# Attention on one core: VectorE's share of the softmax summed in quarters, its polynomial in a scratch tensor, row maxima transposed on VectorE and read earlier

## The reference

```
q, k, v = split_heads(xn @ w.T + b, 16 heads of 16)       # q / sqrt(16)
attn    = softmax(q @ k.T) @ v                            # 4096 x 4096 scores per head
out     = x + (attn @ out_w.T + out_b) + fp8_linear(xn)   # both operands rounded to fp8
```

## Time and profile before

| | |
|---|---|
| median of three runs | 1969.61 us |
| the profiled execution's own time | 1972.75 us |
| its span, first to last instruction | 1970.9 us |
| ScalarE busy | 1820.7 us (92%) |
| TensorE busy | 1916.1 us (97%) |
| VectorE busy | 1276.8 us (65%) |
| granted TensorE clock, mean | 0.990 of full speed |

### The profile page before, as it was taken

How to read it: one execution, slowest core, us unless ns; L and a number is a source line. 1 busy time by engine, 2 the same in 40 slices (tenths; PEclk the granted TensorE clock), 3 DMA queues, 4 the chain that set the end, 5 groups by cost and what they waited for, 6 DMA issues and landing times.

```text
span 1970.9 us, 37661 instructions
## 1 busy us (share of the span) xinstructions
PE 1916.1 (97%) x13945; PEld 663.5 (34%) x13945; DVE 1276.8 (65%) x1789; ACT 1820.7 (92%) x2004; POOL 38.1 (2%) x53
## 2 busy tenths in 40 slices
PE   6969999999999999999999999999999999999979
PEld 4623333333333333333333333333333333333327
DVE  6645766656566766657566766667565766666656
ACT  2339999999999999999999999999999999999983
POOL 2000000000000000000000000000000000000000
PEclk9979999999999999999999999999999999999999
DMA  6870121203030121203030121202030121212022
GB/s 197 272 245 8 20 31 25 31 9 47 9 43 13 17 30 25 31 15 41 9 47 9 17 30 25 31 18 38 9 47 9 17 31 25 30 20 36 9 42 86
DMA packets 65622, 83.70 MB, mean 42 GB/s; under 512 B 9952, under 2 KB 47360, under 8 KB 62208
## 3 DMA queue, kind: packets, MB, share of 16 engines
q1 hardware_dynamic: 65472, 81.58, 20.3%
HBM read 54.79 MB, written 26.21 MB: 41 GB/s over the span
## 4 chain that ended last, share of the span: by engine, by line
PE 94%; DVE 2%; SPq 2%; DMA 1%; issue 1%; ACT 0%; ACTq 0%; DVEq 0%
PE banks L1087 49%; PE banks L1066 36%; PE banks L1094 3%; PE banks L977 1%; PE banks L1202 1%; DVE o_sb L801 1%; PE banks L988 1%; DMA k_parts<-probs 1%; PE banks L1024 1%; SPq L380 0%; PE banks L1044 0%; SPq L340 0%; PE banks L1186 0%; PE banks L1193 0%; PE banks L961 0%
## 5 line engine op out<-in xcount | busy, mean ns | idle before, releaser
L584 ACT ACTIVATE probs<-banks 128x1024 f32<-128x1024 f32 x1923 | 1770.2, 1174 | 13.9 <-PE banks L1066 6.3
L1087 PE MATMUL banks<-probs,v_st 128*32 128x512 f32 x7680 | 1027.1, 607 | 3.2
L1066 PE MATMUL banks<-q_st,k_st 50*128 50x512 f32 x4102 | 818.2, 457 | 6.9 <-ACT probs L584 4.5
L1066 PEld LDWEIGHTS banks<-q_st,k_st 50*128 50x128 f32 x4102 | 369.5, 184 | 809.2 <-ACT probs L584 779.8
L835 DVE SCALAR_TENSOR_TENSOR d_probs<-d_probs,bits 128x1024 f32<-128x1024 f32 x256 | 314.8, 1229 | 8.8
L820 DVE TENSOR_SCALAR bits<-banks 128x512 int32<-128x512 f32 x256 | 177.1, 692 | 187.5 <-PE banks L1066 171.4
L1087 PEld LDWEIGHTS banks<-probs,v_st 128*32 128x32 f32 x7680 | 151.3, 108 | 314.3 <-issue 252.7
L801 DVE STREAM_TRANSPOSE o_sb<-banks 128x512 f32<-128x512 f32 x32 | 22.9, 717 | 260.7 <-PE banks L1087 260.7
L831 DVE SCALAR_TENSOR_TENSOR d_probs<-bits 128x1024 f32<-128x1024 f32 x128 | 157.0, 1226 | 41.7 <-PE banks L1094 38.4
L838 DVE SCALAR_TENSOR_TENSOR d_probs<-d_probs,powers 128x1024 f32<-128x1024 f32 x128 | 156.8, 1225 | 4.4
L826 DVE TENSOR_SCALAR bits<-bits 128x1024 int32<-128x1024 int32 x128 | 88.9, 694 | 4.4
(11 more groups left out here) (91 smaller groups left out, 482.1 us busy)
## 6 DMA issues: line engine op xcount, KB each, us to landing
k_st<-k_parts SPq DMA_DIRECT2D x204, 128.0 KB, 4.3
q_st<-q_parts SPq DMA_DIRECT2D x204, 64.0 KB, 5.0
q_parts<-probs SPq DMA_DIRECT2D x9, 512.0 KB, 6.3
k_parts<-probs SPq DMA_DIRECT2D x9, 512.0 KB, 6.4
xnT_copy<-probs SPq DMA_DIRECT2D x8, 512.0 KB, 4.4
probs<-xnT_copy SPq DMA_DIRECT2D x8, 512.0 KB, 6.8
w_f<-xnT_copy SPq DMA_DIRECT2D x16, 256.0 KB, 5.2
out_dram<-qt SPq DMA_DIRECT2D x16, 256.0 KB, 2.1
```

Source lines behind the costliest of these rows:

```text
L584: act.activation(probs[:, at:at + WIDE * CHUNK].rearrange("p (t c) -> p t c", t=WIDE), banks[:, bank:bank + WIDE, :], ACT.Exp, scale=1.0 / ...
L1066: return pe.matmul(out, k_mm[rows, kt * P:(kt + 1) * P], blocks[rows, qb // GROUPS], start=True, stop=True)
L1087: last = pe.matmul(banks[VCOLS * qb:VCOLS * (qb + 1), 6, :], v_st[:, kt, :], probs[:, at:at + CHUNK], start=first_one, stop=last_one, tile ...
```

## The change

The VectorE blocks are summed in four pieces of 128 columns, not two of 256. The second block's last two tiles move from e = 30 and 36 to 38 and 40, and the maxima from 38 and 40 to 34 and 36; VectorE reads them before the second block's last half. VectorE itself transposes the negated maxima in blocks of 32 x 32, TensorE's transpose is gone, and `neg_row` now holds them in four groups of 32 partitions, which takes 16 DMAs per unit. The polynomial works in a scratch tensor, and only its last step writes `d_probs`.

```
-    ROW_LOADS = 16 * GROUPS * PARTS
+    BLOCKS = P // (PARTS * UT)
+    ROW_LOADS = 16 * GROUPS * PARTS * BLOCKS
-    D_SLOTS = ((2, 4, 6, 14), (16, 24, 30, 36))
-    D_SUM = ((23, 27), (51, 53))
+    D_SLOTS = ((2, 4, 6, 14), (16, 24, 38, 40))
+    D_PIECES = 4
+    D_SUM = ((23, 25, 27, 29), (49, 51, 53, 55))
-    MAX_SLOTS, MAX_TURN = (38, 40), 48
+    MAX_SLOTS = (34, 36)
+    BEFORE_MAX = 3 * QB // 2
...
+        horner = sb("horner", [P, HALF])
+        qt = [horner[:, 0:CHUNK], horner[:, CHUNK:HALF], o_junk]
...
+        def d_job(c, n):
+            return n if c.full or n < BEFORE_MAX else n + c.max_jobs
... load_rows, SyncE
-                        sp.dma_start(q_st[at:at + 1, ...], neg_row[i * UT + g * GT:i * UT + (g + 1) * GT, :])
+                        to = q_st[at:at + 1, u * UG:(u + 1) * UG].rearrange("o (t b x) -> o b t x", t=GT, x=PARTS * UT)
+                        for b in range(BLOCKS):
+                            first_row = b * PARTS * UT + r0
+                            sp.dma_start(to[:, b], neg_row[first_row:first_row + GT, :]).then_inc(c.row_in[u], 16)
... minus_maxima, VectorE
+                    chain(dve.tensor_tensor(neg[:, 1, :].bitcast(F32R), neg_full[:, :], neg[:, 0, :], ALU.subtract),
+                          link0 + 3)
+                    dve.transpose(neg_row[:, :], neg[:, :, :].rearrange("p a t -> p (a t)")).then_inc(c.row_ready, 1)
... d_exponentials: the first three polynomial steps write horner, then
+                    if d and not half:
+                        dve.wait_ge(c.pv_done, h * STEPS + (PV_0 + u * KT + SUM_OF_D[d - 1] + 1))
+                    dve.scalar_tensor_tensor(out=result, in0=horner[:, :], scalar=POLY[3], in1=powers[:, :], ...)
... attend, VectorE, for each unit
+                    d_exponentials(h, 0, 1, 0, job + d_job(c, 4))
+                    if not c.full:
+                        maxima(job + BEFORE_MAX, lk)
+                    d_exponentials(h, 0, 1, 1, job + d_job(c, 6))
... weighted_sum, TensorE
-                        cols = slice(half * (CHUNK // 2), (half + 1) * (CHUNK // 2))
+                        cols = slice(piece * (CHUNK // D_PIECES), (piece + 1) * (CHUNK // D_PIECES))
... one_head, TensorE
-                            jobs[u * UE + MAX_TURN] = (
-                                lambda u=u: turn_maxima(job_of[u] + (D_JOBS + c.max_jobs), h * 2 + (2 + u)))
```

More of the change, by code:

```diff
@@ L145, in program @@
         mpart = sb("mpart", [P, S // CHUNK])
-        neg = sb("neg", [P, P // UT, UT])
+        neg = sb("neg", [P, PARTS, UT])
         neg_full = sb("neg_full", [P, UT])
-        neg_row = sb("neg_row", [PARTS * UT, P])
+        neg_row = sb("neg_row", [P, PARTS * UT])
         o_sb = sb("o_sb", [P, CHUNK])
@@ L268, in program @@
             SUM_ORDER += [(e, i, None, None, kt) for i, kt in enumerate(A_ROWS) if exp_of(QB * i + QB - 1) == e]
-            SUM_ORDER += [(e, None, d, half, D_ROWS[d]) for d in range(len(D_ROWS)) for half in range(2)
-                          if D_SUM[d][half] == e]
-        WHOLE = [(i, d) for _, i, d, half, _ in SUM_ORDER if half != 0]
+            SUM_ORDER += [(e, None, d, piece, D_ROWS[d]) for d in range(len(D_ROWS)) for piece in range(D_PIECES)
+                          if D_SUM[d][piece] == e]
+        WHOLE = [(i, d) for _, i, d, piece, _ in SUM_ORDER if piece in (None, D_PIECES - 1)]
         SUM_OF_A = {i: pos for pos, (i, _) in enumerate(WHOLE) if i is not None}
         SUM_OF_D = {d: pos for pos, (_, d) in enumerate(WHOLE) if d is not None}
+        def d_job(c, n):
+            return n if c.full or n < BEFORE_MAX else n + c.max_jobs
         def ring_user(tile):
@@ L747, in attend @@
             def attend(c):
-                MAX_LINKS = 2 + c.full * UT
+                MAX_LINKS = 3 + c.full * UT
                 SUM_LINKS = 2 if c.full else 3
@@ L828, in d_exponentials @@
                     dve.wait_ge(c.d_chain, steps + 2)
-                    if d and not half:
-                        dve.wait_ge(c.pv_done, h * STEPS + (PV_0 + u * KT + SUM_OF_D[d - 1] + 1))
-                    dve.scalar_tensor_tensor(out=result, in0=bits[:, :], scalar=POLY[0], in1=bits[:, :],
+                    dve.scalar_tensor_tensor(out=horner[:, :], in0=bits[:, :], scalar=POLY[0], in1=bits[:, :],
                                              op0=ALU.add, op1=ALU.mult).then_inc(c.d_chain, 1)
@@ L834, in d_exponentials @@
                         dve.wait_ge(c.d_chain, steps + (2 + j))
-                        dve.scalar_tensor_tensor(out=result, in0=result, scalar=POLY[j], in1=bits[:, :],
+                        dve.scalar_tensor_tensor(out=horner[:, :], in0=horner[:, :], scalar=POLY[j], in1=bits[:, :],
                                                  op0=ALU.add, op1=ALU.mult).then_inc(c.d_chain, 1)
                     dve.wait_ge(c.d_chain, steps + D_STEPS)
-                    dve.scalar_tensor_tensor(out=result, in0=result, scalar=POLY[3], in1=powers[:, :],
+                    if d and not half:
+                        dve.wait_ge(c.pv_done, h * STEPS + (PV_0 + u * KT + SUM_OF_D[d - 1] + 1))
+                    dve.scalar_tensor_tensor(out=result, in0=horner[:, :], scalar=POLY[3], in1=powers[:, :],
                                              op0=ALU.add, op1=ALU.mult).then_inc(c.d_ready, 1)
@@ L875, in attend @@
                     maxima(0, 0)
-                JOB0 = c.max_jobs + 1
+                JOB0 = c.max_jobs
                 with dve.Fori(0, HEADS) as h:
@@ L879, in attend @@
                     lk = h * HEAD_LINKS + MAX_LINKS
[L880 to L884, removed]
+                    d_exponentials(h, 0, 0, 0, job + d_job(c, 0))
+                    d_exponentials(h, 0, 0, 1, job + d_job(c, 2))
+                    d_exponentials(h, 0, 1, 0, job + d_job(c, 4))
+                    if not c.full:
+                        maxima(job + BEFORE_MAX, lk)
+                    d_exponentials(h, 0, 1, 1, job + d_job(c, 6))
+                    if c.full:
+                        maxima(job + QB * len(D_ROWS), lk)
                     take_sums(h, 0, lk + MAX_LINKS)
@@ L887, in attend @@
                     job = job + c.unit_jobs
[L888 to L891, removed]
                     lk = lk + (MAX_LINKS + SUM_LINKS)
-                    maxima(job + QB * len(D_ROWS), lk)
+                    d_exponentials(h, 1, 0, 0, job + d_job(c, 0))
+                    d_exponentials(h, 1, 0, 1, job + d_job(c, 2))
+                    d_exponentials(h, 1, 1, 0, job + d_job(c, 4))
+                    if not c.full:
+                        maxima(job + BEFORE_MAX, lk)
+                    d_exponentials(h, 1, 1, 1, job + d_job(c, 6))
+                    if c.full:
+                        maxima(job + QB * len(D_ROWS), lk)
                     if not c.full:
                         dve.wait_ge(xq_in, h * 16 + 16)
+                        dve.wait_ge(c.d_ready, (h + 1) * (UNITS * len(D_ROWS) * 2))
                         qn[0] = 0
@@ L921, in _ @@
                 attend(second)
-                dve.wait_ge(second.misc_free, HEADS * second.head_jobs + second.max_jobs + 1)
+                dve.wait_ge(second.misc_free, HEADS * second.head_jobs + second.max_jobs)
                 dve.sem_inc(pass2_end, 1)
@@ L1039, in all_max_jobs @@
                                       start=True, stop=True).then_inc(c.misc_full, 1)
[L1041 to L1044, removed]
                 def scores(h, e, before_unit=None):
@@ L1076, in weighted_sum @@
                 def weighted_sum(h, u, n):
-                    e, i, d, half, kt = SUM_ORDER[n]
+                    e, i, d, piece, kt = SUM_ORDER[n]
                     first_one, last_one = n == 0, n == len(SUM_ORDER) - 1
@@ L1096, in weighted_sum @@
                                              stop=False, tile_position=(0, VCOLS * qb))
-                    if half != 0:
+                    if piece in (None, D_PIECES - 1):
                         last.then_inc(c.pv_done, 1)
@@ L1132, in one_head @@
                                 jobs[u * UE + e] = (
-                                    lambda u=u, d=d, qb=qb: d_scores(h, u, d, qb, job_of[u] + (QB * d + qb)))
+                                    lambda u=u, d=d, qb=qb: d_scores(h, u, d, qb, job_of[u] + d_job(c, QB * d + qb)))
                         if not c.full:
                             for g, e in enumerate(MAX_SLOTS):
-                                jobs[u * UE + e] = lambda u=u, g=g: max_part(1 - u, g, job_of[u] + D_JOBS, h * 2 + (2 + u))
-                            jobs[u * UE + MAX_TURN] = (
-                                lambda u=u: turn_maxima(job_of[u] + (D_JOBS + c.max_jobs), h * 2 + (2 + u)))
+                                jobs[u * UE + e] = lambda u=u, g=g: max_part(1 - u, g, job_of[u] + BEFORE_MAX, h * 2 + (2 + u))
                     def maximum_first(u, nxt):
-                        j0 = job_of[1 - u] + D_JOBS
+                        j0 = job_of[1 - u] + QB * len(D_ROWS)
```

(5 more changed lines are left out.)

34 lines of the change are left out of this document (6 added, 28 removed).

## The result

| | before | after |
|---|---|---|
| median of 19 runs each, same chips | 1972.28 us | 1982.34 us |
| ratio, 95% interval | | 1.0049 [1.0038, 1.006] |
| profiled execution's own time, span | 1972.75, 1970.9 | 1985.79, 1984.0 |

What follows compares the result with a forecast made beforehand. ScalarE's exponentials, 0.917 us a step, were taken as the bound. Main stage +4.5 and prologue +4.8 make +9.3 on 1972.75, 1982.0, or 1979 as a median; range 1964.5 to 1988, the forecast's own 1974 to 1984.

Steps and rivals of the forecast that it cites:

- ScalarE's pace of 0.917 us: Main stage: each exponential step takes ScalarE 0.917 us at its own pace; 1923 steps make 1763 us.
- The limit of 1.18 on the lag: Lag: from step e's end to TensorE starting scores for e+3, at even e; above about 1.18 us ScalarE starves.
- quarters that keep under it: TensorE's sums at 0.22 us a quarter keep the lag at most 1.17; both stalls go, -9.9 us alone.
- the rival of quarters bound by instructions: TensorE's sums: 0.30 us a quarter, main stage +12.5, with the prologue +17.3, 1987; chance 0.12, shared with VectorE late at 49.
- the stalls: ScalarE's gaps by steps 31 (0.13 us) and 57 (0.18): 0.31 a unit, 9.9 us over 32 units.
- The wait for the keys at slot 34: Unit 1's earlier maxima wait 0.9 us for the next head's first keys, in all 16 heads.
- The stretch from the first to the last exponential: Main stage: +4.5 us, as 16 x (0.9 - 0.62), instead of -9.9.
- The prologue: Sixteen row DMAs instead of four delay the saves gating the first exponential: +4.8 us, range +2.7 to +5.2.
- the two bounds of the earlier trace: Prologue saves: landed 3.8 us after issue in an empty queue, 6.4 in a full one.
- VectorE in time at step 49: Block 1's last tile, from slot 40, fits by 0.1 us before TensorE's first quarter: costs nothing.
- The scratch tensor at nothing: VectorE's polynomial: same operations, wait moves to the last one where sums are done; VectorE isn't the bound: nothing.

Runs made afterwards that it cites:

- experiment 2: Changed kernel, but unit 1's maxima read the next head's first 32 keys from a small buffer of their own: 1964.31 us, ratio 0.9968.
- experiment 4: Changed kernel with own key buffer for unit 1's maxima and, in the prologue, first rows by TensorE's transpose and four DMAs: 1964.14 us, ratio 0.9946.
- experiment 10: Changed kernel with own key buffer for unit 1's maxima and first rows by four DMAs, measured a second time: 1962.01 us, ratio 0.9943.
- experiment 7: Kernel before plus quarters and the scratch tensor; slots, TensorE's transpose and four row DMAs as before: 1966.74 us, ratio 0.9961.
- experiment 5: Kernel before plus the quarters alone; tiles, maxima, TensorE's transpose and four row DMAs stay: 1986.74 us, ratio 1.0063.
- experiment 6: Changed kernel with the small key buffer and the blocks' sums again in halves at 23, 27, 51, 53: 1974.01 us, ratio 0.9997.
- experiment 1: Changed kernel with the maxima two steps earlier still, at 32 and 34, nothing else: 2050.34 us, ratio 1.0393.
- experiment 3: Changed kernel, but in the prologue the first rows go by TensorE's transpose, VectorE's copy and four DMAs: 1981.69 us, ratio 1.0046.
- experiment 9: Changed kernel with first rows by the old way and four DMAs, a second time beside the changed kernel: 1983.03 us, ratio 1.0041.

## Why the prediction was right, point by point

- *ScalarE's pace of 0.917 us is the floor.* Right and shown: in experiments 2, 4 and 10 no unit after the first takes anything but 55.00, which is 60 steps of 0.917.
- *The limit of 1.18 on the lag, and quarters that keep under it.* Right, and the working too: read from the starts of TensorE's scores in the changed trace, the median lag of unit 0 is 0.78 at step 24, 1.14 at 30, 0.79 at 34, 1.16 at 42 and 0.93 at 56, where 0.78, 1.14, 0.79, 1.17 and 0.91 were worked out. A quarter costs 0.22 to 0.23; the rival of quarters bound by instructions, at 0.30, is out. The limit itself came out at 1.20: a lag of 1.25 lost 0.05 (experiment 7), one of 1.48 lost 0.28 (experiment 5). Halves bring the stalls back (experiment 6).
- *The wait for the keys at slot 34.* Right. 0.9 was said, 0.99 is the mean; slots 1.83 us earlier lengthen it by 1.6 (experiment 1), and removing it returns the unit to 55.00 (experiment 2). ScalarE's loss in unit 1 is 0.94 in the mean, so nearly the whole wait is paid. The stretch from the first to the last exponential grew by 4.6 us; said were 4.5. That the two are so close is in part luck: the fifteen heads after the first grew by 5.2 (0.35 each, where 0.28 was said), and head 0 was 0.6 shorter, though its unit 1 lost as much as the others. Its unit 0 had the clock at 0.50 for 2 us less (last section), which the change doesn't explain.
- *The prologue.* +4.8 was said, +4.3 measured. The sixteen took 11.1 us as worked out (11.2). The gating save was issued 0.4 later than worked out and landed 5.1 after that, halfway between the two bounds of the earlier trace rows, where the forecast stood near the upper one: the term was too large by 0.5. Of three pairs of runs two show it in the time as well (0.0022 and 0.0020 of the ratio) and one doesn't (0.0003); in each the intervals overlap.
- *VectorE in time at step 49.* Right, and by about the 0.1 that was given: in unit 0 of the head shown VectorE ends block 1 at 1081.50 and TensorE loads its first quarter at 1081.66. Over the run TensorE's loads of that quarter are put down to VectorE's last step 32 times, with 9.6 us in all, 0.30 each, which is also the idle time before every other quarter (143.6 in 480). It is the last releaser and costs nothing.
- *The scratch tensor at nothing.* Right for a change that has it. What it covers wasn't asked, and it depends on the slots. With those of the kernel before it covers a wait of 3.1 us a unit, and experiments 5 and 7 price that at 0.0102 of the ratio, 20 us. With the slots of the change no run is without it. VectorE's timeline after, in unit 0 of the same head, shows what stands behind it there: the first step into scratch, the step that writes `d_probs`, and the reading of the maxima.
```profile
1061.52 1.23 DVE L827 SCALAR_TENSOR_TENSOR horner<-bits 128x1024 f32<-128x1024 f32 x1
...
1065.40 1.23 DVE L836 SCALAR_TENSOR_TENSOR d_probs<-horner,powers 128x1024 f32<-128x1024 f32 x1
...
1070.45 0.69 DVE L785 TENSOR_REDUCE mcol<-banks 128x16 f32<-128x512 f32 x1 [3.82 <-PE banks L1027]
```
Without the scratch the first step would start behind the last quarter, at about 1064.6, an estimate from that quarter's start at 1064.10 and the 0.47 us that lay between the two in experiment 5. That is 3.1 us later, and less than the 3.8 us and more that VectorE, as it is, waits for the maxima in every unit. So in this kernel the scratch may well be worth nothing, because the maxima and tiles moved too; that isn't tested.

## What to carry to other kernels

Where one engine sets the pace, look for the gaps between its ends, not at the busy shares: they name the steps and bound all that can be had. Then carry the other engine's lag through the new order by hand; a step moved earlier takes along every wait in it, and the transfer behind it has to be moved as well, or given a small copy of its own. An edit that makes a consumer later holds the producer's buffer longer, so check who writes it next.

## What was not expected of the hardware

The clock. A wait of 0.99 us at slot 34 costs about its own length, and the clock stood at 1.00 through all 16 of them; a wait of 2.6 costs its length in four heads and 3 to 8 us on top in twelve, because TensorE then runs at 0.50 of full speed, 1.2 GHz, for a while (experiment 1). The same explains why unit 0 of head 0 takes 60.95 to 62.15 us in eight of the twelve traces and 56.15 to 56.25 in four. In the eight the clock stays at 0.50 until 17 to 19 us after the first exponential, in the four until under 6. The first stretches of attention in the kernel before and in the run of experiment 10, columns as above:
```profile
144.00:148.00 4.00, 4.00 (x19) 1.35 (x17) 3.87 (x4) 1.94 (x2) 0.00 (x0) 0.50 0.00 0
148.00:152.00 4.00, 4.00 (x20) 1.03 (x22) 1.92 (x2) 2.41 (x3) 0.00 (x0) 0.57 0.00 0
...
144.00:148.00 4.00, 4.00 (x30) 1.28 (x26) 2.87 (x5) 3.90 (x5) 0.00 (x0) 1.00 0.22 66
148.00:152.00 4.00, 4.00 (x32) 1.24 (x28) 3.90 (x4) 4.00 (x5) 0.00 (x0) 1.00 0.00 0
```
Behind the waits of the prologue TensorE starts attention at 1.2 GHz; in the one it is still there at 148 us, in the other it is back at 2.4 GHz by 144. That is 5 us that the same kernel has or has not: the kernel of experiments 3 and 9 took 61.01 and 56.22 for that unit, the one of 4 and 10 61.54 and 56.15. With the first stretch, which varies by 5 us too, it makes up most of what the traces of one kernel differ by. What decides between the two was not tried.
